# Attention operands split into fp16 halves before the transpose, and transposed by DMA instead of TensorE

## The chip, the core and the metric

The kernel runs on one core of a Trainium2 chip. The metric is the device time of one execution in microseconds (us). A core has five engines that run at the same time, each through its own list of instructions in order: TensorE (PE in the profile, with its weight loads as PEld), VectorE (DVE), ScalarE (ACT), GpSimd (POOL) and SyncE (SP), which only issues transfers here. Engines wait for each other through semaphores. SBUF is the on-chip memory (128 partitions), PSUM the accumulation memory into which TensorE writes.

## The reference, cut to what matters

The inputs are 8 sequences of 128 tokens with width 256, and as many context tokens. One layer is computed: layer norm, attention of the 128 tokens to 128 context tokens and (causally) to themselves, with 16 query heads in 4 groups that share a key and value head, then an expert layer.

```python
q = rms_norm((x @ wq).reshape(B, L, 16, 128), q_norm_w)      # likewise k (4 heads), k_ctx
q = q * cos + rotate_half(q) * sin                            # rotated query
scores = einsum('blhd,bmhd->bhlm', q, k_full) * scale + mask  # k_full: context keys, then own keys
probs = softmax(scores, axis=-1)
out = einsum('bhlm,bmhd->blhd', probs, v_full)
x = x + out.reshape(B, L, 2048) @ wo
x = x + moe(layernorm(x))                                     # 8 experts, 2 per token, and a shared one
```

## The kernel before, in words

All matrix products of the attention are made in fp16 but keep nearly fp32 accuracy: an operand is split into a high half (its fp16 rounding) and a low half (fp16 of what is left), and a product is the sum of three: high by high, low by high, high by low. ACT makes the high half, as a copy with a scale (function `copy`, line 435), and DVE the low half, as scale times source minus high half (function `low`, line 879).

The attention is a loop over the 8 sequences (`row(b, first, last)`, one for each engine; rows 1 to 6 are a hardware loop) and in it over the four groups g of four heads. One such step, 32 in all, is called a group step below; u = 4b + g counts them. What runs for a group, spread over neighbouring steps:

- `q(b, g)` projects the query two steps ahead: six matmuls of 512 columns into a PSUM bank. DVE `q_turn` multiplies by cosine and sine (lines 870, 872), GpSimd `q_add` adds the two parts into `q_rot` (line 744), ACT `q_squares` sums the squares for the RMS norm, GpSimd `q_roots` takes the root by a power (line 701).
- PE `q_turn` transposes `q_rot` in fp32, four 128x128 blocks, into the bank `turn` (line 1246). ACT `q_copy` and DVE `q_low` read it and write `qT_hi` and `qT_lo`.
- `scores(b, g)`: twelve matmuls of 256 columns and four that add the mask (lines 1267, 1289), into `sc_ps`. DVE `scores_max` reduces (line 941), ACT `exps` writes `probs` with the row sums, four activations (line 524). The root mean square of q goes into the exponent's scale. DVE `normalise` multiplies the four blocks of `probs` by the reciprocal sums (line 953).
- One step later PE `turn_probs` transposes `probs` in fp32, eight blocks (line 1300), into the two banks `pt_ps`; ACT `p_copy` and DVE `p_low` make `pT_hi` and `pT_lo`.
- `mix` multiplies them with the values (six matmuls of 512 columns, line 1310) at the end of that step; ACT `o_copy` and DVE `o_low` split the output.

Beside this, once in a row: step 0 projects the context values and the values (`vc`, `v`), step 1 carries the output projection of the row before (`out_proj`, 48 matmuls of 256 columns, line 1324) and transposes the next inputs (`turn_inputs`), step 2 projects the next row's context keys and keys (`kc`, `k`), whose norms go ACT `kc_squares`, GpSimd `kc_roots`, ACT `kc_scale`, ACT `k_squares`, GpSimd `k_roots` and `k_scale`, and step 3 transposes them on PE (`kc_turn`, `k_turn`); ACT `kc_copy` and `k_copy` and DVE `kc_low` and `k_low` split them. In step 0 the ACT order after the exponentials is `q_squares`, `v_copy`, `o_copy`, `vc_copy`; DVE `vc_low` releases the bank into which PE projects the query of group 3 (`q`, which waits for `vc_ready`), ahead of `out_proj` on PE's list.

The order on each engine is written out by hand. SP's queue holds the loads of the weights at the start, the load of `wo` (2 MB, line 406, when the last part of `wq` has been split), one load of 128 KB of context per row and two of 1 MB of expert weights, and the stores at the end.

## Time and profile before

| what | value |
|---|---|
| median of 3 runs | 377.71 us (375.49 to 378.03) |
| profiled execution, its own time | 377.97 us |
| its span, first to last instruction | 376.3 us |
| mean granted TensorE clock | 0.977 of 2.4 GHz |
| PE, DVE, ACT, POOL busy | 91%, 87%, 72%, 44% of the span |
| bytes moved by DMA | 13.49 MB |

Instructions have durations that overlap their neighbour's on the same engine by some 0.1 us, so the distance between two starts is the better price; both are used below and named. "Idle before" is the time an engine stood still ahead of the group, with what released it. Registers, branches, semaphores and the issue of DMAs do not count as busy.

### The profile page before, as it was taken

What the parts mean: (1) busy time and instruction counts of PE and PEld (TensorE: products, weight loads), DVE (VectorE), ACT (ScalarE), POOL (GpSimd) and SP (SyncE); (2) the same over time, 40 slices, a digit from 0 to 9 for tenths busy, and PEclk for the clock granted to TensorE, in tenths of its full rate; (3) what the DMA queues carried; (4) which work ended last, traced back from release to release, by engine and by line L of the source; (5) the groups of instructions that cost most, each with busy time, mean ns of one, the idle gap of its engine ahead of it and who ended that gap; (6) DMA issues with size and microseconds to landing.
All of it is one profiled execution on the core that took longest, in us unless ns stands there. A gap on an engine that the chain in (4) does not pass through costs nothing.

```text
span 376.3 us, 7781 instructions
## 1 busy us (share of the span) xinstructions
PE 343.7 (91%) x2471; PEld 237.3 (63%) x2476; DVE 325.6 (87%) x625; ACT 271.2 (72%) x913; POOL 165.8 (44%) x242
## 2 busy tenths in 40 slices
PE   6697798799999999999999999999999999998994
PEld 5373555376567665866685577567666778674572
DVE  1668999998999899899989998999899897759653
ACT  3557879676986797699759876986797567167562
POOL 3356565652754275427344443644174300334330
PEclk9788989999999999999999999999999999989999
DMA  5967000000030003000000000000000000000011
GB/s 179 379 212 223 17 0 2 1 2 14 3 111 0 14 0 111 14 1 0 0 14 0 0 0 14 0 0 0 0 0 1 2 0 2 2 0 3 22 35 57
DMA packets 11603, 13.49 MB, mean 36 GB/s; under 512 B 824, under 2 KB 9024, under 8 KB 11584
## 3 DMA queue, kind: packets, MB, share of 16 engines
q1 hardware_dynamic: 11584, 13.25, 11.0%
q8 instruction: 10, 0.16, 0.2%
q14 instruction: 9, 0.07, 0.1%
HBM read 12.20 MB, written 1.05 MB: 35 GB/s over the span
## 4 chain that ended last, share of the span: by engine, by line
PE 40%; DVE 24%; ACT 17%; issue 10%; POOL 4%; DMA 2%; SPq 1%; DVEq 1%; ACTq 0%; POOLq 0%
PE proj L1324 10%; ACT probs L524 8%; PE pt_ps L1300 5%; DVE probs L953 5%; PE proj L1157 4%; PE turn L1246 3%; DVE nmax L941 3%; DVE pT_lo L879 3%; PE o_ps L1310 3%; POOL q_rot L744 3%; PE sc_ps L1267 2%; ACT pT_hi L435 2%; DMA wq<-in_L_xattn_wq_dram 2%; ACT q_junk L468 2%; DVE q_t L870 2%
## 5 line engine op out<-in xcount | busy, mean ns | idle before, releaser
L524 ACT ACTIVATE probs<-sc_ps,nbias,q_r 128x256 f32<-128x256 f32 x128 | 70.8, 574 | 2.8 <-DVE nbias L945 2.8
L744 POOL TENSOR_TENSOR q_rot<-q_t 128x512 f32<-128x512 f32 x32 | 41.4, 1295 | 42.8 <-DVE q_t L872 42.0
L953 DVE TENSOR_SCALAR probs<-probs,rden 128x256 f32<-128x256 f32 x128 | 51.2, 461 | 1.1
L1157 PE MATMUL proj<-wq_hi,xT 128*128 128x512 f16 x128 | 40.1, 396 | 2.9 <-DVE wq_lo L863 2.9
L435 ACT ACTIVATE pT_hi<-pt_ps 128x512 f16<-128x512 f32 x64 | 34.8, 597 | 10.9 <-PE pt_ps L1300 10.9
L468 ACT ACTIVATE q_junk<-proj 128x128 bf16<-128x128 f32 x128 | 34.0, 295 | 11.7 <-DVE q_t L872 11.7
L879 DVE SCALAR_TENSOR_TENSOR pT_lo<-pt_ps,pT_hi 128x512 f16<-128x512 f32 x64 | 41.0, 682 | 0.6 <-ACT pT_hi L435 0.6
L941 DVE TENSOR_REDUCE nmax<-sc_ps 128x4 f32<-128x1024 f32 x32 | 38.9, 1214 | 1.5 <-PE sc_ps L1289 1.5
L831 POOL TENSOR_TENSOR wq<-xn_all,weight 128x512 bf16<-128x512 f32 x16 | 17.1, 1074 | 44.1 <-DVE weight L1098 23.4
L1324 PE MATMUL proj<-wo_hi,oT_hi 128*128 128x256 f16 x128 | 34.9, 273 | 0.0
L1324 PE MATMUL proj<-wo_lo,oT_hi 128*128 128x256 f16 x128 | 34.9, 273 | 0.0
L1324 PE MATMUL proj<-wo_hi,oT_lo 128*128 128x256 f16 x128 | 34.9, 273 | 0.0
L1300 PE MATMUL pt_ps<-ident,probs 128*128 128x128 f32 x256 | 34.2, 278 | 0.3
L701 POOL TENSOR_TENSOR q_r<-q_me,power 128x4 f32<-128x4 f32 x32 | 33.3, 1042 | 2.5
L435 ACT ACTIVATE qT_hi<-turn 128x512 f16<-128x512 f32 x32 | 19.5, 610 | 19.9 <-PE turn L1246 19.9
L1300 PEld LDWEIGHTS pt_ps<-ident,probs 128*128 128x128 f32 x256 | 29.5, 143 | 0.8 <-DVE probs L953 0.5
L1246 PE MATMUL turn<-ident,q_rot 128*128 128x128 f32 x128 | 19.8, 277 | 10.6 <-POOL q_rot L744 4.9
L468 ACT ACTIVATION_READ_ACCUMULATOR q_junk<-proj 128x1 f32 x128 | 28.5, 227 | 0.0
L524 ACT ACTIVATION_READ_ACCUMULATOR probs<-sc_ps,nbias,q_r 128x1 f32 x128 | 27.6, 215 | 0.0
L1310 PE MATMUL o_ps<-pT_hi,v_hi 128*128 128x512 f16 x64 | 24.3, 379 | 3.2 <-DVE pT_lo L879 3.2
L879 DVE SCALAR_TENSOR_TENSOR oT_lo<-o_ps,oT_hi 128x512 f16<-128x512 f32 x32 | 21.9, 686 | 5.8 <-ACT oT_hi L435 5.8
L1267 PE MATMUL sc_ps<-kT_hi,qT_hi 128*128 128x256 f16 x128 | 24.5, 273 | 0.5 <-ACT probs L524 0.2
(216 smaller groups left out, 920.7 us busy)
## 6 DMA issues: line engine op xcount, KB each, us to landing
wq<-in_L_xattn_wq_dram SPq DMA_DIRECT2D x4, 512.0 KB, 9.1
w<-in_L_ffn_w_dram SPq DMA_DIRECT2D x2, 1024.0 KB, 10.5
wq<-in_L_xattn_wo_dram SPq DMA_DIRECT2D x1, 2048.0 KB, 8.2
ctx_b<-in_ctx_dram SPq DMA_DIRECT2D x8, 128.0 KB, 2.1
out_dram<-x_all SPq DMA_DIRECT2D x4, 256.0 KB, 2.2
x_all<-in_x_dram SPq DMA_DIRECT2D x1, 896.0 KB, 12.3
wkc<-in_L_xattn_wk_ctx_dram SPq DMA_DIRECT2D x1, 512.0 KB, 4.2
wk<-in_L_xattn_wk_dram SPq DMA_DIRECT2D x1, 512.0 KB, 5.1
```

The lines of the kernel that those rows point to most:

```text
L435: return nc.scalar.activation(out_, in_, ACT.Copy, scale=scale)
L468: last = nc.scalar.activation(junk[:, head], bank[:, head], ACT.Square, scale=scale, accum_out=dst[:, h:h + 1])
L524: last = nc.scalar.activation(probs[:, h, :], sc_ps[:, h, :], ACT.Exp, bias=nbias[:, h:h + 1], scale=q_r[:, g, h:h + 1], accum_out=den[:, ...
L701: nc.gpsimd.tensor_tensor(r, me, power[:], ALU.pow).then_inc(root, 1)
L744: nc.gpsimd.tensor_tensor(q_rot[:], q_t1[:], q_t2[:], ALU.add).then_inc(q_added, 1)
L879: return nc.vector.scalar_tensor_tensor(out=lo, in0=src, scalar=scale, in1=hi, op0=ALU.mult, op1=ALU.subtract)
L941: nc.vector.tensor_reduce(nmax[:], sc_ps[:], AX_X, ALU.max, negate=True).then_inc(s_max, 1)
L953: last = nc.vector.tensor_scalar(probs[:, h, :], probs[:, h, :], rden[:, h:h + 1], None, ALU.mult)
L1157: last = nc.tensor.matmul(bank[:], xT[:, a, c, :], w[:, c, cols], start=(n == 0), stop=(n == 3 * DC - 1))
L1300: last = nc.tensor.transpose(pt_ps[:, a, h * P:(h + 1) * P], probs[:, h, a * P:(a + 1) * P], ident[:])
L1310: last = nc.tensor.matmul(o_ps[:], v[:, a, g * P:(g + 1) * P], p[:, a, :], start=(a == 0 and i == 0), stop=(a == 1 and i == 2))
L1324: last = nc.tensor.matmul(proj[0][:, 0:D], o[:, h // R, (h % R) * P:(h % R + 1) * P], w[:, h, :], start=(h == 0 and i == 0), stop=(h == H ...
```

## The change

Both fp32 operands are split where they lie, before they are transposed, and the fp16 halves are then transposed by DMA (SBUF to SBUF, issued from SP): per group step two transfers for the query (128x512 fp16 each) and four for the probabilities (high and low of two pairs of heads, 128x512 fp16 each), 192 in all. The transposes of PE at lines 1246 and 1300 go. `p_split` on ACT now multiplies by the reciprocal sums and rounds in one, and `p_rest` on DVE makes the low half from `probs`; so `normalise` goes, and `inv_den` computes the reciprocals and their scale. ACT `q_copy` reads `q_rot`; the low half of the query goes from DVE to GpSimd (`q_rest`), as does `k_add`. The transposed probabilities have two slots. `kc_copy` and `k_copy` move from the middle of the exponentials to their end, `kc_squares` moves behind `p_split`, `mix` of step 0 moves behind `v`. The load of `wo` is cut in four, two ahead of the first transposes and two behind the first probabilities; those of `w3` and `w2` are cut in four too.

```diff
@@ SP @@
+            def turn_q(b, g):
+                seen(sp, s_done, u)
+                for src, dst, split, landed in ((q_hi, qT_hi, q_high, d_qT_hi), (q_lo, qT_lo, q_low, d_qT_lo)):
+                    sp.wait_ge(split, u + 1)
+                    sp.dma_start_transpose(dst[:].rearrange("p (h t) -> p h t", h=R), src[:]).then_inc(landed[g % 2], 16)
+            def turn_probs(b, g):
+                if u >= 2:
+                    sp.wait_ge(pv_done, u - 1)
+                for pair in range(2):
+                    for src, dst, split in ((p_hi, pT_hi, p_high), (p_lo, pT_lo, p_low)):
+                        sp.wait_ge(split, 2 * u + 1 + pair)
+                        sp.dma_start_transpose(dst[:, slot, heads, :, :].rearrange("p h a t -> p (h a) t"),
+                                               src[:, heads, :].rearrange("p h k -> p (h k)")).then_inc(d_pT[slot][pair], 16)
+            sp.wait_ge(w_lo, G + 1)
+            load_wo(0)
+            load_wo(1)
+            turn_q(0, 0)
+            for b in range(B):
+                for g in range(G):
+                    if ahead_of(b, g, 1, b == B - 1):
+                        turn_q(*ahead_of(b, g, 1, b == B - 1))
+                    turn_probs(b, g)
+                    if (b, g) == (0, 0):
+                        load_wo(2)
+                        load_wo(3)
...
@@ ACT @@
             def q_copy(b, g):
-                act.wait_ge(q_turned, G * b + g + 1)
-                copy(qT_hi[:], turn[:], Q_SCALE / XW).then_inc(q_high, 1)
+                act.wait_ge(q_added, G * b + g + 1)
...
+                copy(q_hi[:], q_rot[:]).then_inc(q_high, 1)
+            def p_split(b, g):
+                act.wait_ge(s_rden, G * b + g + 1)
+                for pair in range(2):
...
+                    for h in (2 * pair, 2 * pair + 1):
+                        last = copy(p_hi[:, h, :], probs[:, h, :], rden[:, h:h + 1])
+                    last.then_inc(p_high, 1)
             def row(b, first, last):
-                    if g or not first:
-                        p_copy(u - 1)
-                    exps(b, g, (kc_copy, k_copy) if g == 3 and not last else ())
+                    exps(b, g)
...
+                    if g == 3 and not last:
+                        kc_copy(b + 1)
+                        k_copy(b + 1)
+                        p_split(b, g)
+                    if ahead_of(b, g, 2, last):
+                        q_squares(*ahead_of(b, g, 2, last))
+                    if g != 3 or last:
+                        p_split(b, g)
                     if g == 2 and not last:
                         kc_squares(b + 1)
-                    if ahead_of(b, g, 2, last):
-                        q_squares(*ahead_of(b, g, 2, last))
@@ POOL @@
+            def q_rest(b, g):
+                pool.wait_ge(q_high, G * b + g + 1)
...
+                nc.gpsimd.tensor_tensor(q_lo[:], q_rot[:], q_hi[:], ALU.subtract).then_inc(q_low, 1)
             def row(b, first, last, cast=None):
                 for g in range(G):
+                    if ahead_of(b, g, 1, last):
+                        q_rest(*ahead_of(b, g, 1, last))
...
                     if g == 2 and not last:
+                        k_add(b + 1)
                         k_roots(b + 1)
                         k_scale(b + 1)
                         q_roots(b + 1, 0)
@@ DVE @@
+            def inv_den(b, g):
+                nc.vector.reciprocal(inv[:], den[:]).then_inc(s_inv, 1)
+                dve.wait_ge(s_inv, u + 1)
+                nc.vector.tensor_scalar(rden[:], inv[:], P_SCALE, None, ALU.mult).then_inc(s_rden, 1)
+            def p_rest(b, g, pair):
+                dve.wait_ge(p_high, 2 * u + 1 + pair)
+                for h in (2 * pair, 2 * pair + 1):
+                    last = low(p_lo[:, h, :], probs[:, h, :], rden[:, h:h + 1], p_hi[:, h, :])
+                last.then_inc(p_low, 1)
             def row(b, first, last):
-                    if ahead_of(b, g, 1, last):
-                        q_low(*ahead_of(b, g, 1, last))
-                    if g or not first:
-                        p_low(u - 1)
                     if ahead_of(b, g, 2, last):
                         q_turn(*ahead_of(b, g, 2, last))
+                    inv_den(b, g)
+                    p_rest(b, g, 0)
...
                     if g == 3 and not last:
                         kc_low(b + 1)
                         k_low(b + 1)
-                    normalise(b, g)
+                    p_rest(b, g, 1)
@@ PE @@
             def scores(b, g):
-                pe.wait_ge(q_high, u + 1)
+                pe.wait_ge(d_qT_hi[g % 2], qT_landed(b, g))
...
-                        pe.wait_ge(q_ready, u + 1)
+                        pe.wait_ge(d_qT_lo[g % 2], qT_landed(b, g))
             def row(b, first, last):
-                    if ahead_of(b, g, 1, last):
-                        q_turn(*ahead_of(b, g, 1, last), last)
-                    if g or not first:
-                        turn_probs(b, g)
```

## Rows read from the trace of the kernel before

**Rows 1.** Page, part 1: busy us of each engine, share, instructions

```profile
PE 343.7 (91%) x2471; PEld 237.3 (63%) x2476; DVE 325.6 (87%) x625; ACT 271.2 (72%) x913; POOL 165.8 (44%) x242
```

**Rows 2.** Stretches: length; busy PE, PEld, DVE, ACT, POOL; clock, DMA share, GB/s

```profile
193.85:229.50 35.65, 34.39 (x249) 23.90 (x248) 33.99 (x68) 28.34 (x107) 15.90 (x24) 1.00 0.02 4
...
46.00:50.00 4.00, 2.22 (x13) 2.18 (x14) 3.96 (x6) 2.85 (x4) 4.00 (x2) 0.78 0.00 0
```

**Rows 3.** Groups by line, taken away: busy us, mean ns of one | idle

```profile
L953 DVE TENSOR_SCALAR probs<-probs,rden 128x256 f32<-128x256 f32 x128 | 51.2, 461 | 1.1
...
L879 DVE SCALAR_TENSOR_TENSOR pT_lo<-pt_ps,pT_hi 128x512 f16<-128x512 f32 x64 | 41.0, 682 | 0.6 <-ACT pT_hi L435 0.6
...
L435 ACT ACTIVATE pT_hi<-pt_ps 128x512 f16<-128x512 f32 x64 | 34.8, 597 | 10.9 <-PE pt_ps L1300 10.9
```

**Rows 4.** Groups by line: the nearest rows to what it adds

```profile
L435 ACT ACTIVATE x_hi<-xs 128x256 f16<-128x256 f32 x8 | 3.5, 434 | 2.9 <-DVE xs L858 2.9
...
L879 DVE SCALAR_TENSOR_TENSOR cT_lo<-turn,cT_hi 128x256 f16<-128x256 f32 x7 | 3.0, 423 | 0.0
...
L712 POOL TENSOR_TENSOR x_lo<-xs,x_hi 128x256 f16<-128x256 f32 x8 | 5.4, 670 | 27.5 <-ACT x_hi L435 27.5
...
L930 DVE TENSOR_TENSOR k_sum<-k_t 128x512 f32<-128x512 f32 x8 | 8.4, 1053 | 0.0
```

**Rows 5.** Chain that ended last, in order of time (start, us, what): PE's step 1

```profile
221.25 1.29 PE proj L1157 x6
...
222.55 5.24 PE proj L1324 x48
...
228.24 1.29 PE o_ps L1310 x6
...
229.53 0.98 PE sc_ps L1267 x9
...
231.51 0.89 PE pt_ps L1300 x8
```

**Rows 6.** Timeline of steps 2 to 3 (start us, us, engine, line)

```profile
195.59 1.23 DVE L941 TENSOR_REDUCE nmax<-sc_ps 128x4 f32<-128x1024 f32 x1 [0.21 <-PE sc_ps L1289]
...
197.87 0.57 ACT L524 ACTIVATE probs<-sc_ps,nbias,q_r 128x256 f32<-128x256 f32 x1
...
199.94 0.23 ACT L524 ACTIVATION_READ_ACCUMULATOR probs<-sc_ps,nbias,q_r 128x1 f32 x1
...
201.34 0.31 POOL L699 TENSOR_TENSOR kc_me<-kc_ss,eps_kc 128x4 f32<-128x4 f32 x1 [6.71 <-ACT kc_junk L468]
...
202.79 1.14 ACT L435 ACTIVATE kc_n<-turn,kc_r 128x128 f32<-128x128 f32 x4
...
205.10 0.20 POOL L699 TENSOR_TENSOR k_me<-k_ss,eps_k 128x4 f32<-128x4 f32 x1 [1.11 <-ACT k_junk L468]
...
206.52 1.04 POOL L730 TENSOR_TENSOR k_rot<-k_sum,k_r 128x512 f32<-128x512 f32 x1
...
208.94 1.26 POOL L744 TENSOR_TENSOR q_rot<-q_t 128x512 f32<-128x512 f32 x1
...
209.40 0.38 PE L1267 MATMUL sc_ps<-kT_hi,qT_hi 128*128 128x256 f16 x2
```

**Rows 7.** Page, part 6 and part 3: DMA issues to landing, and packets

```profile
ctx_b<-in_ctx_dram SPq DMA_DIRECT2D x8, 128.0 KB, 2.1
...
wq<-in_L_xattn_wo_dram SPq DMA_DIRECT2D x1, 2048.0 KB, 8.2
...
q1 hardware_dynamic: 11584, 13.25, 11.0%
```

**Rows 8.** Timeline: the issue of `wo`, the first scores, the last maximum

```profile
29.25 0.38 SPq L406 DMA_DIRECT2D wq<-in_L_xattn_wo_dram  x1
...
26.49 0.38 PE L1267 MATMUL sc_ps<-kT_hi,qT_hi 128*128 128x256 f16 x2
...
308.02 1.21 DVE L941 TENSOR_REDUCE nmax<-sc_ps 128x4 f32<-128x1024 f32 x1
```

More of the change, by code:

```diff
@@ L216, in xattn_moe_kernel @@
         d_wvc = sem("d_wvc")
-        d_wo = sem("d_wo")
+        d_wo = [sem(f"d_wo{i}") for i in range(4)]
         d_tab = sem("d_tab")
@@ new lines, in _ @@
+            sp.wait_ge(w_lo, G + 1)
[10 more added lines that the diff above has]
+                        load_wo(3)
+                    if g == 1 and b + 2 < B:
+                        next_ctx(b + 2)
+                    for load, r in ((load_w3, 1), (load_w2, 2)):
+                        if (b, g) in ((r, 1), (r, 2)):
+                            load(g - 1)
+                        if (b, g) == (r + 1, 0):
+                            load(2)
+                            load(3)
@@ L528, in exps @@
                 last.then_inc(s_exp, 1)
-            def p_copy(u):
-                act.wait_ge(p_turned, u + 1)
-                for a in range(2):
-                    copy(pT_hi[:, a, :], pt_ps[:, a, :], P_SCALE).then_inc(p_high, 1)
             def o_copy(u, g):
@@ L724, in k_roots, with k_add @@
                 inv_rms(k_ss[:], k_me[:], k_r[:], eps_k, k_sq, k_mean, k_root, nb + 1)
+            def k_add(nb):
+                pool.wait_ge(k_t12, nb + 1)
+                seen(pool, k_norm, nb)
+                nc.gpsimd.tensor_tensor(k_sum[:], k_t1[:], k_t2[:], ALU.add).then_inc(k_added, 1)
             def k_scale(nb):
@@ L755, in _ @@
             kc_roots(0)
+            k_add(0)
             k_roots(0)
@@ L759, in _ @@
             q_roots(0, 0)
+            q_rest(0, 0)
             q_add(0, 1)
@@ L899, in k_low @@
                     kT_hi[:, :, 1, :]).then_inc(k_ready, 1)
-            def q_low(b, g):
-                dve.wait_ge(q_high, G * b + g + 1)
-                low(qT_lo[:], turn[:], Q_SCALE / XW, qT_hi[:]).then_inc(q_ready, 1)
             def vc_low(b):
@@ L1001, in _ @@
             k_low(0)
-            q_low(0, 0)
             q_turn(0, 1)
@@ L1059, in row @@
                         o_low(u - 1, (g - 1) % G)
-                    if g == 2 and not last:
-                        k_add(b + 1)
                     if g == 0:
@@ L1410, in row @@
                         vc(b)
-                        if not first:
-                            mix(u - 1, G - 1)
-                        else:
+                        if first:
                             pe.wait_ge(w_lo, G + 2)
                         v(b)
+                        if not first:
+                            mix(b - 1, G - 1)
                     if g == 1:
```

185 lines of the change are left out of this document (87 added, 98 removed).

## The prediction

> **What bounds the kernel now.** I read the busy times first. PE has 343.7 us of 376.3 and DVE 325.6 [rows 1]; in one turn of the hardware loop, 35.65 us, PE is busy 34.39, DVE 33.99, ACT 28.34 and GpSimd 15.90 [rows 2]. So two engines are full and a third is at 80%. The chain that ended last says how they are coupled: in step 1 it stays on PE (query projection 1.29 us, output projection 5.24, mix 1.29, then the scores) [rows 5], and in steps 2 to 0 it goes through ACT, GpSimd and DVE. The reader should see in the timeline that step 2 is a relay: exponentials on ACT until 200.17, key norms on GpSimd from 201.34, `kc_n` on ACT from 202.79, GpSimd again from 205.10, `k_rot` from 206.52, and the next row's first scores on PE at 209.40 [rows 6]. An engine with less to do shortens a row only if the relay gets shorter too.
>
> **The change by engine, for one row.** PE loses 4 x 8 transposes of probabilities at 0.89 us per eight [rows 5] and 4 x 4 of the query at half that: 4 x 1.34 = 5.3 us, down to 29.1. DVE loses four pairs of `pT_lo` (8 x 0.68), four `qT_lo` of the same form (2.7), sixteen blocks of `normalise` (16 x 0.46 = 7.4) and `k_sum` (1.05) [rows 3, 4]; it gains sixteen low halves of 128x256. The nearest row is the low half of the context at 0.42 us [rows 4], which reads PSUM; both inputs now lie in SBUF. From below 0.33 (an overlap of 0.1 taken off), from above 0.63, since `k_sum` shows 1.05 for 512 elements from SBUF and half of that plus an overlap is that [rows 4]. I take 0.42: 6.8, and 0.7 for the scale of the reciprocals. DVE ends at 34.0 - 16.6 + 7.5 = 24.9. ACT loses eight `pT_hi` (8 x 0.60 = 4.8 [rows 3]) and gains sixteen 128x256 copies at 0.43 [rows 4], 6.9: up to 30.4; spaced start to start I take 0.31 each, 1.25 for a step's four. GpSimd gains four low halves of the query (twice `x_lo`, 1.3 us [rows 4]) and `k_add`: up to 22.
>
> So every engine sums to less than 31 us where a row now takes 35.5. That is the promise. The work is now nearly balanced on four engines with ACT on top, and what decides is the relay.
>
> **The relay after the change**, with the start of step 2's scores as 0; before, it is at 193.85 and the next row's at 229.5 [rows 2, 5]. Scores 1.7, maximum and bias 1.4, exponentials 2.3 (197.87 to 200.17 [rows 6]): 5.5, where it was 6.3, because ACT no longer has `pT_hi` ahead. Then ACT runs `q_squares` 1.0, **`p_split` 1.25** and only now `kc_squares` 1.0: 8.75. GpSimd's norm takes 1.5 (201.34 to 202.79 [rows 6]): 10.25, where ACT has already finished `o_copy` and waits. `kc_scale` and `k_squares`, 2.05: 12.3. It was 11.1 (205.10 less 193.85, less a hand-over). GpSimd: `k_roots` 1.45, `k_scale` 1.0, `q_roots` 1.35 and then, at the head of its step 3, **`q_rest`** 1.3, the low half of the next row's first query: 17.4. Behind it stand `q_add` and the roots of the next query. The low half must now cross a **DMA**: the plain load of 128 KB takes 2.1 us from issue to landing [rows 7]. Transposes are not in this trace. From below I take the bytes' rate, 2 MB in 8.2 us, or 0.5 us for 128 KB [rows 7]; from above 3.9, that load's 2.1 and 1.8 for smaller packets (worked out under (a)). I take 2.1, the row with the same size and issuer: 19.6. PE has waited for it since 16.6: `k_turn` could start at 14.8, behind `k_scale`, and takes 0.5, `mix` 1.3. Six score matmuls of 0.11 and the rest of the scores, 0.9: 21.2. Before, these scores started at 209.40, which is 15.55, and ended at 17.5 [rows 6].
>
> DVE alone would give 1.3 less: `p_split(3)` stands behind `k_copy`, which waits for `k_turn` (15.3), so the first `p_high` comes at 16.7, and DVE has `p_rest`, `kc_low`, `k_low`, `p_rest` and `o_low` (3.2) ahead of the maximum.
>
> Maximum and bias 1.5, exponentials 2.3: 25.0, where it was 22.1. ACT `q_squares` 1.0, `p_split` 1.25, `v_copy`, `o_copy`, `vc_copy` 0.5 each: 28.8. DVE `v_low`, `o_low` and `vc_low` end at 29.7, and that is what PE waits for before the query projection of group 3: 1.3, output projection 5.25, inputs 0.45, mix 1.3 [rows 5]: **38.1 for the row, against 35.5**. The four transposes' cover on PE is gone at this point, so their 1.3 us of step 1 brings nothing: PE stood waiting for DVE anyway. Six loop rows: +15.6 us. In row 0 DVE also has the splits of `wo`, so I count +1 there.
>
> What else the edits cost. `mix` has the transfers of the probabilities ahead of it; in step 0 the last is issued at 19.4 and PE comes at 25 (21.2 and three projections), so 5 us of landing cost nothing. Two slots make the reuse free. The reciprocals' scale is 0.2 us on DVE before `p_split`, beside `q_squares` on ACT. `k_add` (1.05 to 1.3) lies beside `kc_scale` on ACT. The pieces of `w3` and `w2` run beside compute as now.
>
> **The start.** SP issues half of `wo` first and then the first query. The issue of `wo` is at 29.25 [rows 8], some 1.1 earlier with DVE's two operations less; half of 2 MB takes 4.1 [rows 7], a transfer behind it 2.1: 34.4, against scores at 26.49 [rows 8]. PE's next work (query, context values, values) is then later by 4 to 5 us, as the next scores had waited for other things. I take +5, between 2 (DVE catches up) and 9. The last row has no keys to make and gains 2; its tail has PE work to cover the last transfers.
>
> The sum: 377.97 (the profiled execution, 0.3 above the median) + 15.6 + 1 + 5 - 2 = 397.6, so 398. A row could also be worth +1 (the query's low half finds GpSimd free earlier) or +4.5 (3.9 us landing, DVE slowed by GpSimd's reads): 387 to 414 for this case.
>
> **TensorE's clock.** PE would stand idle for over 3 us twice in a row (before the query projection that waits for `k_squares`, and before the scores, from 16.6). In this trace PE had 2.2 us of work in the 4 us from 46, and the granted clock was 0.78 there, against 1.00 in the loop row [rows 2]; part of that stretch ran at 1.2 GHz. It is in the upper bound above, since PE has slack in those steps.
>
> **The rivals.**
>
> (a) The transfers become the bound. A row has 24 of them, and they go through one queue in order: at 38.1 us per row the point is 1.59 us for one. Bulk bytes give 0.5. By packets it is 1.8: 11584 packets took 11.0% of 16 engines' 376.3 us [rows 7], 57 ns each, and 128x512 in pieces of 256 bytes is 512 packets, 32 an engine. Then 192 x 1.8 = 346, plus 30 before the first (the first scores at 26.5 and the half of `wo`) and 63 behind the last (the last maximum is at 308.0 [rows 8], its halves 5 later): 439. Each further 0.2 us adds 38. If one 128x128 block cost a whole plain transfer's 2.1 without overlap, it would be 192 x 8.4 = 1613 plus 93, 1706 us. Against (a) stands that SP is held only 0.38 us by the issue of a plain transfer, even one of 2 MB [rows 8]. The Trainium skill speaks on both sides. "DMA: Bandwidth & Descriptors" (Latency and other measured facts) gives DMA transposes 261 GB/s or more, an estimate of 0.5 us each, and (a) would not happen. "VectorE: DVE Perf Modes" (The three transpose paths) gives 1309 ns for one 128x128 block by DMA and advises TensorE where PSUM will do: block by block that is an estimate of 5.2 us per transfer, 192 x 5.2 + 93, 1091 us. No transpose is in this trace, so neither is confirmed. I give 24% for (a), with 5 of these for block by block.
>
> (b) Faster: the relay has more room than I see, and a row is the sum of the largest engine share in each step. PE in step 1 (9.8 with the scores), ACT in step 2 (8.4), 6.8 and 7.1: 32.1, 3.4 less than now. Seven rows: -24, start +5, last row -2: 357. For it speaks that DVE is 96% busy in a row and falls by a quarter; against it, that its relief lies in steps where it then waits for ACT. It decides on whether `q_rest` or `p_split` stands in the chain. 18%, from 352 to 373.
>
> (c) Both effects cancel, within 1% of 377.7: 10%. One percent is about what a measurement can tell from no change.
>
> **The numbers.** The relay case 48%, (a) 24%, (b) 18%, (c) 10%. Prediction 398 us. The range from 364 to 470 leaves out half of (b) and of (a), 2 in 10. Its own range is 387 to 414. Faster by over 1%: 18%, within: 10%, slower: 72%.
>
> **What would show it.** A row of about 38 us in the distance of the maxima of step 2; PE busy below 80% with waits for `qT_lo`'s transfer ahead of step 0's scores and for `v_lo` ahead of group 3's query projection; ACT waiting for `kc_r`; first scores at 33 or later. Wrong if PE's longest waits are on probabilities in every step with the queue busy all the time (a), or if a row is under 35 us (b).

## The result, and the profile after

| | us |
|---|---|
| before, median of 4 | 376.6 (375.45 to 378.03) |
| after, median of 4 | 446.32 (445.32 to 449.9) |
| ratio | 1.1866 [1.1781, 1.1951] |
| span after, mean granted clock | 443.6, 0.887 |

The change makes the kernel 19% slower: the direction that was forecast, at over three times the size (+69.7 us against +20). One run of `x4_qfirst` and one of `x17_two_probs`, each over 1.5% above that kernel's fastest, are left out of their medians below. The page of the changed kernel: busy times (as [rows 1]), the granted clock in 40 slices, the transfers' queue, their time to landing.

```profile
PE 332.8 (75%) x2279; PEld 227.2 (51%) x2284; DVE 289.9 (65%) x553; ACT 288.4 (65%) x977; POOL 213.1 (48%) x283
...
PEclk9968578979887988798889898969996998899999
...
q1 hardware_dynamic: 117712, 38.44, 37.0%
...
pT_hi<-p_hi SPq DMA_TRANSPOSE x64, 2.4
pT_lo<-p_lo SPq DMA_TRANSPOSE x64, 2.4
```

No engine is over 75% busy where two were at 91 and 87%. Two stretches, one loop row and its part from step 3's maximum to step 0's (columns as in [rows 2]):

```profile
196.64:239.30 42.66, 33.24 (x223) 22.50 (x222) 29.41 (x58) 30.51 (x115) 22.29 (x31) 0.88 0.33 72
205.72:217.49 11.77, 8.75 (x45) 5.68 (x46) 7.99 (x14) 9.76 (x37) 9.66 (x12) 0.71 0.31 67
```

Every engine has 9 us or more of idle time in 42.66, PE and ACT included, so the row is made of waits. The longest by sum (engine, line, what it waited for: total us, times, longest):

```profile
ACT probs L589 <- DVE nbias L1020: 71.4, 25, 8.1
DVE p_lo L963 <- ACT p_hi L491: 44.3, 32, 1.9
...
PE proj L1230 <- ACT k_junk L524: 31.1, 8, 4.5
...
PE proj L1230 <- DVE v_lo L963: 25.3, 8, 4.6
...
PE sc_ps L1318 <- DMA qT_lo<-q_lo: 17.9, 15, 2.4
```

The second is the one that the forecast had not priced: in all 32 group steps DVE stands idle for `p_hi`, 1.4 us on average, while its own next maximum is queued behind `p_lo`. The groups that answer to [rows 3, 4] (busy, mean ns | idle before):

```profile
L1230 PE MATMUL proj<-wq_hi,xT 128*128 128x512 f16 x128 | 48.9, 472 | 57.9 <-ACT k_junk L524 31.1
L963 DVE SCALAR_TENSOR_TENSOR p_lo<-probs,rden,p_hi 128x256 f16<-128x256 f32 x128 | 61.6, 532 | 45.6 <-ACT p_hi L491 44.3
L491 ACT ACTIVATE p_hi<-probs,rden 128x256 f16<-128x256 f32 x128 | 55.0, 522 | 1.3 <-DVE rden L1027 1.1
```

The relay of step 2, as [rows 6] (timeline by start; first ACT, then GpSimd, then PE, then SP):

```profile
201.36 1.73 ACT L491 ACTIVATE p_hi<-probs,rden 128x256 f16<-128x256 f32 x4
202.96 0.30 ACT L524 ACTIVATE kc_junk<-turn 128x128 bf16<-128x128 f32 x1
...
205.59 1.14 ACT L491 ACTIVATE kc_n<-turn,kc_r 128x128 f32<-128x128 f32 x4 [0.98 <-POOL kc_r L765]
```

```profile
204.26 0.20 POOL L763 TENSOR_TENSOR kc_me<-kc_ss,eps_kc 128x4 f32<-128x4 f32 x1 [6.80 <-ACT kc_junk L524]
...
211.65 1.16 POOL L820 TENSOR_TENSOR q_lo<-q_rot,q_hi 128x512 f16<-128x512 f32 x1
```

```profile
207.82 1.03 PE L1230 MATMUL proj<-wq_hi,xT 128*128 128x512 f16 x2 [4.49 <-ACT k_junk L524]
...
215.29 0.39 PE L1318 MATMUL sc_ps<-kT_hi,qT_lo 128*128 128x256 f16 x2 [0.81 <-DMA qT_lo<-q_lo]
...
227.98 1.03 PE L1230 MATMUL proj<-wq_hi,xT 128*128 128x512 f16 x2 [3.35 <-DVE v_lo L963]
```

```profile
208.35 1.19 SPq L445 DMA_TRANSPOSE qT_hi<-q_hi  x1
212.83 1.19 SPq L445 DMA_TRANSPOSE qT_lo<-q_lo  x1
214.12 1.22 SPq L456 DMA_TRANSPOSE pT_hi<-p_hi  x1
```

The timeline has the forecast relay in its order: `kc_junk` behind `p_hi`, GpSimd's norm 6.8 us idle before it, the low half of the next row's query issued at 212.83 and used at 215.29. It also has what the relay does to PE: after 4.49 and 3.35 us of standing still, pairs of the query projection take 1.03 us where they took 0.6. The granted clock of this part is 0.71: after the wait TensorE runs at the lower of its two levels (1.2 GHz), and the six matmuls take 2.74 us instead of 1.29.

One more thing in this row was in no term of the forecast's sum. The bias of step 3, `nbias`, takes 1.06 us and that of step 0 takes 0.62, where it takes 0.16 alone; each ends as the GpSimd operation beside it ends (DVE, then GpSimd):

```profile
206.97 1.06 DVE L1020 TENSOR_TENSOR nbias<-nmax,q_r 128x4 f32<-128x4 f32 x1
...
218.74 0.62 DVE L1020 TENSOR_TENSOR nbias<-nmax,q_r 128x4 f32<-128x4 f32 x1
```

```profile
206.75 1.26 POOL L793 TENSOR_TENSOR k_sum<-k_t 128x512 f32<-128x512 f32 x1
...
218.18 1.15 POOL L820 TENSOR_TENSOR q_lo<-q_rot,q_hi 128x512 f16<-128x512 f32 x1
```

Both of these operations are on GpSimd by the change. `rden` is stretched in the same way twice in the row (0.83 and 0.58 for 0.17).

### The profile page after: what moved, and what is told of

The parts are those of the page before. It is cut to its first block, busy times and chain, and to the rows that moved or that the text cites. A ratio compares the mean times of both kernels' runs of the same rounds, so it can differ in the third digit from the quotient of the medians.

```text
span 443.6 us, 7750 instructions
## 1 busy us (share of the span) xinstructions
PE 332.8 (75%) x2279; PEld 227.2 (51%) x2284; DVE 289.9 (65%) x553; ACT 288.4 (65%) x977; POOL 213.1 (48%) x283
## 2 busy tenths in 40 slices
DMA packets 117733, 38.69 MB, mean 87 GB/s; under 512 B 105416, under 2 KB 115664, under 8 KB 117712
## 3 DMA queue, kind: packets, MB, share of 16 engines
q1 hardware_dynamic: 117712, 38.44, 37.0%
HBM read 12.20 MB, written 1.05 MB: 30 GB/s over the span
## 4 chain that ended last, share of the span: by engine, by line
PE 34%; ACT 23%; DVE 22%; issue 9%; POOL 5%; DMA 4%; SPq 2%; DVEq 1%; ACTq 0%; POOLq 0%
PE proj L1370 9%; ACT probs L589 8%; PE proj L1230 7%; ACT p_hi L491 5%; DVE p_lo L963 5%; DVE nmax L1016 5%; PE sc_ps L1318 3%; DMA qT_hi<-q_hi 3%; ACT q_junk L524 3%; PE o_ps L1354 2%; DVE kT_lo L963 2%; DVE v_lo L963 2%; DVE oT_lo L963 2%; ACT k_junk L524 2%; ACT kc_junk L524 2%
## 5 line engine op out<-in xcount | busy, mean ns | idle before, releaser
L963 DVE SCALAR_TENSOR_TENSOR p_lo<-probs,rden,p_hi 128x256 f16<-128x256 f32 x128 | 61.6, 532 | 45.6 <-ACT p_hi L491 44.3
L491 ACT ACTIVATE p_hi<-probs,rden 128x256 f16<-128x256 f32 x128 | 55.0, 522 | 1.3 <-DVE rden L1027 1.1
L1230 PEld LDWEIGHTS proj<-wq_hi,xT 128*128 128x128 f16 x128 | 12.3, 112 | 73.8 <-ACT k_junk L524 32.2
L1016 DVE TENSOR_REDUCE nmax<-sc_ps 128x4 f32<-128x1024 f32 x32 | 38.9, 1217 | 13.1 <-PE sc_ps L1340 13.1
L820 POOL TENSOR_TENSOR q_lo<-q_rot,q_hi 128x512 f16<-128x512 f32 x32 | 37.2, 1163 | 7.3 <-ACT q_hi L491 7.1
L1354 PE MATMUL o_ps<-pT_hi,v_hi 128*128 128x256 f16 x128 | 37.3, 291 | 3.3 <-DVE oT_lo L963 2.7
L1318 PE MATMUL sc_ps<-kT_hi,qT_lo 128*128 128x256 f16 x128 | 25.6, 283 | 17.9 <-DMA qT_lo<-q_lo 17.9
L954 DVE TENSOR_TENSOR q_t<-proj,q_cos 128x512 f32<-128x512 f32 x32 | 22.0, 688 | 23.3 <-PE proj L1230 23.0
L1354 PE MATMUL o_ps<-pT_hi,v_lo 128*128 128x256 f16 x128 | 36.8, 287 | 0.0
L1354 PE MATMUL o_ps<-pT_lo,v_hi 128*128 128x256 f16 x128 | 36.6, 286 | 0.0
L1318 PE MATMUL sc_ps<-kT_lo,qT_hi 128*128 128x256 f16 x128 | 26.2, 285 | 0.8
```

The lines of the kernel that those rows point to most:

```text
L491: return nc.scalar.activation(out_, in_, ACT.Copy, scale=scale)
L820: nc.gpsimd.tensor_tensor(q_lo[:], q_rot[:], q_hi[:], ALU.subtract).then_inc(q_low, 1)
L963: return nc.vector.scalar_tensor_tensor(out=lo, in0=src, scalar=scale, in1=hi, op0=ALU.mult, op1=ALU.subtract)
L1016: nc.vector.tensor_reduce(nmax[:], sc_ps[:], AX_X, ALU.max, negate=True).then_inc(s_max, 1)
L1230: last = nc.tensor.matmul(bank[:], xT[:, a, c, :], w[:, c, cols], start=(n == 0), stop=(n == 3 * DC - 1))
L1318: nc.tensor.matmul(sc_ps[:, h, :], a[:, h * P:(h + 1) * P], w[:, g, :, :].rearrange("p a t -> p (a t)"), start=start, stop=False, skip_gro ...
```

## The experiments

Each ran beside the kernel before (medians 375.5 to 376.8); times are medians, ratios are to it.

**Which half of the change costs it.** `x5_only_p` keeps the query's path of before, `x6_only_q` the probabilities' path of before.

```diff
 x5_only_p: PE q_turn, ACT q_copy from `turn`, DVE q_low as before; no turn_q on SP, no q_rest
 x6_only_q: PE turn_probs, ACT p_copy, DVE normalise and p_low as before; no turn_probs on SP, no p_split
```

> Only the probabilities are split first and transposed by DMA; the query goes the old way (TensorE transposes it, ACT and DVE read PSUM), everything else as in the changed kernel. Relay theory: p_split and p_rest stay in the chain of steps 2, 3 and 0 and the slow clock stays, but the first scores of a row no longer wait for GpSimd's low half and its transfer (0.8 to 2 us a row) and the start no longer waits for a transfer behind wo (8 us): 39.5 to 42 us a row, 415 to 430 us. Rival (the query's path is the whole loss): 385 or less.

> Only the query is split first and transposed by DMA; the probabilities go the old way (normalised, transposed by TensorE, split out of PSUM), everything else as in the changed kernel. Relay theory: the key squares end 1.5 us earlier without p_split, but the query's low half still crosses GpSimd and the queue, and the start is still 7 to 10 us late: 38 to 40.5 us a row, 405 to 425 us. Rival (the probabilities' path is the whole loss): 390 or less.

Measured: 426.87 us, 1.1304 [1.1242, 1.1365], as expected; and 398.97, 1.0582 [1.0531, 1.0632], faster than expected. Less the 376.8 of before that is +50.1 and +22.2, together 72.3 against 69.7 for both: the parts add up, and the probabilities carry some 70%.

**Are the transfers the bound?**

```diff
-for src, dst, split in ((p_hi, pT_hi, p_high), (p_lo, pT_lo, p_low)):
+for src, dst, split in ((p_hi, pT_hi, p_high),):          # 16 transfers a row, not 24
```

> The changed kernel without the transfers of the probabilities' low halves: 16 transposes a row instead of 24 (the third product uses the high half twice, so this leaves out the low half of the probabilities; the split itself is still computed). Queue theory: SP is held 1.26 us by each of 24, 31 of a row's 43 us, and the waits for the query's low half come from standing behind them, so a third less gives 3 to 6 us a row, 405 to 425 us. Relay theory: the query's low half is issued when GpSimd has made it and the probabilities are never late, so a row gains at most 1 us, in step 0, and the kernel 0 to 8: 438 to 446.

Measured: 450.58, 1.1958 [1.1903, 1.2013]. A third of the transfers less gives nothing. Rival (a) is refuted: a transfer behind another holds SP 1.26 us and lands after 2.4, and 24 of them are some 30 us of a 42.66 us row.

**TensorE's clock.** Dummy matmuls into a free bank in PE's two long waits.

```diff
+if g == 1: stay_warm(18)      # ahead of the wait for k_squares
+if g == 3: stay_warm(14)      # ahead of the wait for v_lo
```

> The changed kernel with 18 dummy matmuls of 512 columns ahead of PE's wait for the key squares in step 3 and 14 ahead of its wait for the context values in step 1, both into a PSUM bank that nobody reads there (3.9 and 3.0 us, less than the two stalls of 4.5 and 3.4 us). Clock theory: the two query projections behind the stalls took 2.74 us at 1.2 GHz instead of 1.3, and two groups of transposes 0.87 instead of 0.45; all of it lies in the relay, so a loop row falls from 43.1 us by 2.3 to 2.8, the kernel from 446 to 427 to 431 us, and the mean granted clock rises from 0.887 to above 0.95. Rival (the relay is set by ACT and GpSimd alone, the slow matmuls are hidden): under 4 us less, and a row of 42 or more.

Measured: 438.21, 1.1635 [1.1548, 1.1721], clock 0.948. Half of what was expected. In the loop rows the distance of the maxima of steps 1 and 2, which was 10.2 to 13.1 us, is 10.2 to 10.5 in all of them, but that of steps 3 and 0 rose from 11.8 in most rows to 12.3 to 12.5: PE was earlier there and waited for `qT_lo` instead.

**The order of work.** Four reorderings, alone and together.

```diff
 x2_kcfirst: ACT, step 2:   kc_squares ahead of p_split
 x4_qfirst:  SP, start:     turn_q(0, 0) ahead of load_wo(0), load_wo(1)
 x7_relay:   both, and DVE k_turn, kc_low, k_low ahead of p_rest; GpSimd q_rest ahead of q_roots(b + 1, 0)
 x9_pfirst:  x7_relay, and ACT p_split ahead of q_squares in steps 0 to 2
 x8_relay_warm: x7_relay with 12 and 10 dummies as in x1_warm
```

> The changed kernel with the squares of the context keys ahead of the split of the probabilities on ACT in step 2, so that GpSimd's root runs beside the split. Relay theory: ACT no longer waits 1.0 us for the root, the key squares end 1.0 us earlier, and a row is worth 0.7 to 1.1 us less: 438 to 442 us. Rival (the row is set elsewhere, by the queue of transfers or DVE): no change beyond 1.5 us.

> The changed kernel with the transfers of the first query issued ahead of the two quarters of wo and of the wait in front of them. Theory of the start: the first scores come at 28 to 30 us instead of 32.5, and the gain survives to the end: 441 to 444 us. Rival: PE waits for the context values at 45 us anyway (3.7 us of idle time there), so nothing of it is left: 445 to 447.

> The changed kernel with five moves that shorten the relay and compute the same: ACT squares the context keys ahead of p_split; DVE rotates the keys (k_turn) ahead of p_rest in step 2; DVE makes the keys' low halves ahead of p_rest in step 3; GpSimd makes the next row's first q_rest ahead of its q_roots; the first query's transfers are issued ahead of wo. Relay theory: 1.0 from the squares (now DVE no longer holds them up), 1.3 from q_rest, 0.5 to 1 in step 3, and 6.5 us at the start: 39.5 to 41.5 us a row, 418 to 430 us. Rival (each gain turns into another wait, as the first such move did): above 436.

> The kernel before in this list with 12 and 10 dummy matmuls of 512 columns in PE's two stalls. If order and clock add up: another 1.5 to 2.5 us a row, 38 to 39.5 us, 405 to 418 us, a mean clock above 0.95. If they overlap: within 5 us of the kernel without dummies. In neither case do I expect less than 390, since ACT's p_split and DVE's p_rest remain in the chain.

> The x7_relay kernel (428.9 us) with `p_split` of steps 0 to 2 straight behind the exponentials (and `kc_squares`), ahead of `q_squares`. Theory, the ping-pong of ACT and DVE sets a step: with only the probabilities by DMA, DVE stands 5.9 us of a row idle for `p_hi`, 1.4 to 1.8 in each step, and the next maximum is queued behind its `p_lo`. `q_squares` is 0.9 to 1.0 us of that, so three steps of a row come up to 1 us earlier: rows of 39.5 to 41 where x7_relay has 42.1, 408 to 420 us, and DVE's waits for `p_hi` fall from 4.2 us a row to under 2. Rival, the steps are set by PE's waits for the squares, `kT` and `v_lo`: 425 to 432, DVE's saved wait comes back ahead of the maximum. Rival, the later `q_squares` delays GpSimd's roots and with them the bias: over 430.

Measured: `x2_kcfirst` 445.84, 1.1817 [1.1749, 1.1885], nothing, where 4 to 8 us were expected: the wait moved to DVE, whose `k_turn` stood behind `p_lo`, and ACT's `k_squares` waited 1.70 us for it. `x4_qfirst` 439.13, 1.1648 [1.1559, 1.1738], a little more gain than expected. `x7_relay` 428.91, 1.1354 [1.1288, 1.142], 10 under `x4_qfirst`: with `k_turn`, the keys' low halves and `q_rest` moved too, the swap is part of a gain. No run says which of these moves brought it. `x9_pfirst` 418.71, 1.1151 [1.1115, 1.1186], a further 10, as expected. `x8_relay_warm` 426.02, 1.1323 [1.1244, 1.1403]: the clock is worth at most 3 us once the order is mended (the single runs of the two kernels overlap, 426.0 to 429.9 and 424.8 to 429.9), so as far as these two kernels tell, it was mostly a consequence of the waits. Order and start are 28 of the 70 us.

**The query's half.** First by order, then with the first query of each row turned by PE again, so that no transfer lies between the keys' norm and the next row's scores.

```diff
 x10_q_early: x6_only_q with turn_q(0, 0) ahead of wo, and q_rest ahead of q_roots(b + 1, 0)
 x13_hybrid:  x6_only_q; group 0: PE q_turn, ACT copy and DVE low half from `turn`; groups 1 to 3 by DMA;
              kc_copy and k_copy again amid the exponentials
```

> Only the query by DMA (399.0 us), with two edits: its first transfers go ahead of `wo`, and GpSimd makes the low half of the next row's first query before the roots of its norm. If the relay into the next row is what this half of the change costs (step 3 to step 0 takes 11.9 us there against 7.7 before), the low half comes 1.2 to 1.35 us earlier in each of seven rows, 8 to 9 us, and the start gives the 4 to 7 us it gave in x4_qfirst: 383 to 388 us. Rival, the roots are then late for the bias of step 0 and give it back: 391 to 396 (the start's part alone). Rival, the landing of the transfer, 2.4 us, is counted from the end of `k_scale` anyway and nothing moves but the start: as the first rival.

> Only the query by DMA, but the first query of each row is turned by PE and split from PSUM by ACT and DVE as before, queries 1 to 3 go by DMA, and the two key copies stand amid the exponentials of step 3 as before. PE keeps one of four query turns. If the 22 us of the query's part lie in the relay into the next row and in the start, both are gone: rows 34.5 to 36 where before has 35.5, 370 to 382 us in all, and no wait for a transfer over 0.5 us. If they lie in GpSimd's extra work (three low halves of 1.16 us and `k_add` 1.27 a row, with DVE held beside them), rows stay near 37.9: 390 to 398. PE has 2 us less to do in a row; if PE's work were what bounds the kernel before, this version would be 10 to 14 us faster than it, 363 to 367.

Measured: 385.46, 1.0262 [1.0223, 1.03], and 377.5, 1.0047 [1.0021, 1.0073], both as expected. The start and the place of `q_rest` gave back 13.5 of the query's 22 us. The rest came back with the first query's turn on PE; since `x13_hybrid` also puts the key copies back amid the exponentials, how the 8 us divide between the two isn't shown. A loop row of `x13_hybrid` (columns as above):

```profile
195.86:231.63 35.77, 33.14 (x236) 22.43 (x235) 31.91 (x63) 28.47 (x107) 20.34 (x28) 1.00 0.12 26
```

PE has 1.2 us less to do than in [rows 2], DVE 2.1, and the row is no shorter than 35.65: neither was what set it. The suspect is the keys' relay, of which one link was still late (`kc_squares` behind `q_squares`: it starts 5.4 us behind the maximum of step 2, and 4.5 in the kernel before). The next two change that link, and then take `k_add` off GpSimd.

```diff
 x14_hybrid_kc:  x13_hybrid, ACT step 2: kc_squares ahead of q_squares
 x15_hybrid_add: x14_hybrid_kc, k_add on DVE ahead of step 3's maximum
```

> x13_hybrid (377.5 us) with one swap on ACT in step 2: `kc_squares` ahead of `q_squares`, as in the kernel before. In x13_hybrid the rows are 35.8 us with 2 us less on PE; the first of the context keys' squares starts at 201.23 there against 200.04 before, and step 3 to step 0 takes 9.8 us against 7.7. Theory, the relay of the keys sets the row: each of seven rows comes 0.9 to 1.2 us earlier, 369 to 372 us, about 1.5% under the kernel before. Rival, GpSimd's order (`q_add`, then `k_add`, ahead of the keys' roots) holds the relay anyway: its wait is 0.3 us behind ACT's, so 0.3 us a row are the least that would be left, 375. Rival, the row is set elsewhere: 377.

> x14_hybrid_kc with `k_add` back on DVE, where the kernel before has it (ahead of the maximum of step 3). GpSimd's 1.28 us leave the relay between the two norms; DVE gets 1.2 us. If GpSimd's queue holds the relay by 0.3 to 1.3 us once ACT is earlier: 1 to 5 us under x14_hybrid_kc, 365 to 370. Rival, DVE's maximum of step 3 is then 1.2 us later and holds the exponentials, within which the key copies stand: same as x14_hybrid_kc or up to 4 us slower.

Measured: 369.22, 0.9822 [0.9794, 0.985], and 368.48, 0.9811 [0.9786, 0.9836]. One swap on ACT, which starts `kc_squares` 1.35 us earlier in the row, makes each loop row 1.24 us shorter and the kernel 8.3 us: the keys' relay does set the row. **Both versions beat both kernels**, the one before by 1.8 and 1.9%; what the second adds can't be told from nothing. A row of `x14_hybrid_kc`:

```profile
156.00:190.54 34.54, 33.15 (x236) 22.42 (x235) 32.02 (x64) 28.39 (x107) 21.46 (x30) 1.00 0.13 27
```

**GpSimd beside DVE.** Four spare products (SBUF to SBUF, 128x512, nothing reads them) in GpSimd's idle time of step 2.

```diff
+for i in range(4): nc.gpsimd.tensor_tensor(gp_junk[:, i], q_cos (broadcast), q_sin (broadcast), ALU.mult)
                         kc_roots(b + 1)
```

> The changed kernel (446.3 us) with four spare products of 128x512 on GpSimd in each row's step 2, where it stands idle for about 8 us ahead of the context keys' norm; nothing waits for them unless they outlast that idle time. Each should take 1.0 to 1.3 us. Theory, DVE is held beside GpSimd when both its inputs are in SBUF: `nbias` (0.16 us alone) and the four `p_lo` (1.67 us for four alone) in that stretch last until GpSimd's operation ends, 1 to 3 us longer a row, and those that read PSUM (maximum, `q_t`, `oT_lo`) keep their durations; 452 to 468 us. Rival, DVE's long operations only wait for something else: durations as before and 444 to 449.

> The kernel before (375.8 us) with the same four spare products on GpSimd as x12_gp_after, 5 us in a wait of 6.7. If DVE is held beside GpSimd by any operation without PSUM among its inputs, `nbias` (0.16 us), the second norm (0.41) and possibly `rden` stretch to the end of GpSimd's operation, 0.6 to 1.2 us each, while the maximum, `qT_lo`, `pT_lo` and `q_t`, which read PSUM, keep their durations: 2 us a row, of which DVE's 1.6 us of idle time a row can take some: 378 to 392 us. The kernel before has fewer such operations beside GpSimd than the changed one, so the ratio should be no larger than the 1.018 of x12_gp_after to the changed kernel. Rival, GpSimd's work is free in its idle time: 375 to 377.

Measured: on the changed kernel 454.51, 1.2083 [1.2044, 1.2122]; on the kernel before 386.42, 1.0303 [1.026, 1.0347]. Timeline of the first, GpSimd and DVE:

```profile
200.78 5.00 POOL L862 TENSOR_TENSOR gp_junk<-q_cos,q_sin 128x512 bf16<-128x512 f32 x4
```

```profile
201.26 0.80 DVE L1024 TENSOR_TENSOR nbias<-nmax,q_r 128x4 f32<-128x4 f32 x1
201.99 1.43 DVE L1057 TENSOR_SCALAR xn_all<-x_all,ln_mv,ln_rs  x1
203.34 0.68 DVE L958 TENSOR_TENSOR q_t<-proj,q_cos 128x512 f32<-128x512 f32 x1
...
204.74 1.07 DVE L1031 TENSOR_SCALAR rden<-inv 128x4 f32<-128x4 f32 x1
206.78 1.68 DVE L967 SCALAR_TENSOR_TENSOR p_lo<-probs,rden,p_hi 128x256 f16<-128x256 f32 x4 [0.98 <-ACT p_hi L492]
```

`nbias` takes 0.80 us where it takes 0.16, `xn_all` 1.43 for 0.41, `rden` 1.07 for 0.17; `q_t`, with one input in PSUM, keeps its 0.68, and `p_lo`, behind GpSimd's last product, its 1.68. The three that are stretched have all their inputs in SBUF, and each ends as one of GpSimd's four products ends (1.25 us each). So they are held by GpSimd, and what reads PSUM and the reciprocal are not. The size of it in the row: loop rows of 43.6 us on average where the changed kernel has 43.1, 2.7 over five rows. In row 0 the products outlast GpSimd's idle time of 2.9 us, and the keys' norm starts 2.9 us later behind the maximum, so the 8 us aren't all the price of held operations. The expectation for the kernel before came out in number but not in place: its loop rows are 35.7 us against 35.5, and 9 us are lost between the maxima of step 2 of row 0 and of row 1 (45.13 to 94.91, against 48.16 to 88.94 before). There GpSimd isn't idle ahead of the keys' norm: the norm starts 12.0 us behind the maximum, where it started 6.9 behind it, so the products push it back by their own 5 us. This run's ratio, the larger one against the expectation, therefore says little on held operations; its durations do.

**The probabilities' half.** The same reorderings with only the probabilities by DMA; then two buffers for `probs`, so that `p_lo` leaves the path to the next maximum; then no `p_lo` at all.

```diff
 x16_p_early:   x5_only_p; kc_squares, then p_split right behind exps; k_turn, kc_low, k_low ahead of p_rest
 x17_two_probs: x16_p_early; probs[2]; p_rest(u - 1) behind scores_max(u); exps(u) waits for p_rest(u - 2);
                p_split(u) waits for p_rest(u - 1), since p_hi has one buffer
 x18_no_rest:   x16_p_early; no p_rest, no pT_lo; mix reads pT_hi a third time
```

> Only the probabilities by DMA (426.9 us) with the order of work of x9_pfirst where it bears on them: `kc_squares` and then `p_split` straight behind the exponentials, `k_turn` and the keys' low halves ahead of `p_rest`. If the loss of the probabilities' half is the ping-pong ACT, DVE, ACT of each step, most of the 5.9 us of a row in which DVE waits for `p_hi` goes: rows of 38 to 39.5 where it has 41.2, 402 to 414 us, and what is left (25 us and more over before) is the 1.7 us of `p_hi` and 1.7 of `p_lo` in series in every step against normalise alone at 1.14. Rival, TensorE's clock (0.93 there) and its waits are the cause and not the order: 420 or more.

> x16_p_early (425.4 us, only the probabilities by DMA) with two buffers for `probs`: DVE makes `p_lo` of a step behind the next step's maximum and bias, and the next exponentials no longer wait for it. In x16_p_early the scores of step 3 are done at 185.5 and the maximum starts at 188.15, behind four `p_lo` that took 3.68 us beside two operations of GpSimd; in step 0 the scores are done at 203.3 and the maximum starts at 206.94. Theory, the loss of the probabilities' half is `p_hi` on ACT and `p_lo` on DVE in series between the exponentials of one step and the maximum of the next: the maxima start as their scores are done, rows of 37 to 39.5 where x16_p_early has 40.9, 395 to 415 us. Rival, the low halves are then late for `mix` (2.5 us of transfer behind them), and PE waits for transfers where DVE waited for ACT: 418 to 435.

> x16_p_early (425.4 us) without the low half of the probabilities at all: neither `p_lo` on DVE nor its transfers; `mix` uses the high half in its place, so PE's work is the same. The exponentials wait for `p_hi` alone. It takes 8.7 us a row off DVE (33.8 of 40.9 busy there; four `p_lo` of 1.67 to 3.68) and 8 of 16 transfers. Theory, the row is the ring of ACT and DVE (maximum, exponentials, `p_hi`, `p_lo`, maximum) : most of one `p_lo` per step comes off, rows of 34 to 37, 380 to 400 us. Rival, what is left is `p_hi` on ACT in the same ring, the waits of PE for `kT` and `v_lo` and its clock, and DVE's work fits beside: 408 or more. x3_noplo, which took away the transfers alone, changed nothing, so the two together are DVE's part.

Measured: `x16_p_early` 425.44, 1.1315 [1.1279, 1.1352], a miss: nothing gained. `x17_two_probs` 462.8, 1.2265 [1.2151, 1.2379], a miss the other way, by its rival's mechanism but far beyond its range: the low halves and their transfers are then late for `mix`, in one row PE waits 3.2 us for `pT_lo`, and DVE 4.3 and 5.1 for `v_hi` and `oT_hi`. ACT's `p_hi` also waits there, 3.9 us for the reciprocals and 1.9 for a landing, so this run doesn't test the ring by itself. `x18_no_rest` 404.28, 1.0738 [1.0697, 1.078], between its two cases. In `x16_p_early` DVE's waits for `p_hi` did fall, from 5.9 to 2.4 us a row, but (its DVE, then GpSimd in that stretch):

```profile
183.94 3.68 DVE L931 SCALAR_TENSOR_TENSOR p_lo<-probs,rden,p_hi 128x256 f16<-128x256 f32 x4
187.55 0.68 DVE L931 SCALAR_TENSOR_TENSOR oT_lo<-o_ps,oT_hi 128x512 f16<-128x512 f32 x1
188.15 1.21 DVE L988 TENSOR_REDUCE nmax<-sc_ps 128x4 f32<-128x1024 f32 x1
```

```profile
184.10 1.45 POOL L794 TENSOR_TENSOR q_rot<-q_t 128x512 f32<-128x512 f32 x1
185.50 1.44 POOL L774 TENSOR_TENSOR k_sum<-k_t 128x512 f32<-128x512 f32 x1
```

Four `p_lo` take 3.68 us instead of 1.67: moved earlier, they fell beside two operations of GpSimd and gave the 2 us back, while step 3's scores had been done since 185.5. That this is why nothing was gained is argued from the trace and not shown: in `x5_only_p` `nbias` of step 3 is held instead (1.07 us), which is 0.16 here, so the net is 1 us. The rows of `x5_only_p` and `x18_no_rest`:

```profile
179.16:220.35 41.19, 32.81 (x240) 22.86 (x239) 31.19 (x62) 30.63 (x115) 18.13 (x26) 0.96 0.23 53
```

```profile
170.49:208.40 37.91, 31.34 (x240) 22.45 (x239) 23.53 (x47) 30.39 (x115) 17.90 (x26) 1.00 0.13 31
```

Taking out `p_lo` and its transfers (which alone are worth nothing, `x3_noplo`) gives 21 us of the 49. The other 28 stay with DVE at 23.5 us of 37.9: they aren't DVE's work. In this row PE still waits 2.6 us for `v_lo`, whose `v_hi` stands behind `p_hi` and `q_squares` on ACT, and 1.4 for `kc_n`. That `p_hi` in ACT's queue is the cause of all 28 is argued from these waits, not shown by a run.

## Why the prediction was right in direction and wrong in size

**Right.** The relay: `p_split` ahead of `kc_squares`, and GpSimd's `q_rest` and a transfer ahead of the next row's scores. With the scores' start as 0 (194.91 here), the exponentials end at 5.45 (forecast 5.5), `kc_squares` at 9.05 (8.75), `k_squares` at 12.69 (12.3), the query's low half lands at 20.4 (19.6), the next row's scores end at 22.1 (21.2). The removal of PE's work gives nothing, and rival (b) is refuted beyond the kernel itself: `x13_hybrid` has less work on PE and DVE in a row, and the same row. (c) and (a) are refuted too, (a) by `x3_noplo`. The landing of 2.1 us, taken from the plain load, was near: 2.4.

**Wrong: the size, in four terms.** By the maxima of step 2, the span of the profiled executions grew by 67.3: 10.3 up to row 0, 8.9 to row 1, 37.9 in five loop rows (35.54 to 43.1 each), 4.7 to row 7 and 5.6 behind it. Forecast were 5, 3.6, 13, and -2 for the last.

The step that failed is the sum of the relay from the next row's scores on. In the row shown, 42.66 us where the sum had 38.1, the 4.6 that it lacks are 0.9 up to the end of those scores (22.1 for 21.2), 2.4 from there to `vc_low` (10.9 for 8.5) and 1.3 from `vc_low` to the next step 2 (9.7 for 8.4). The sums by engine came out for ACT (30.51, forecast 30.4) and GpSimd (22.29, forecast 22), not for DVE (29.41, forecast 24.9) and PE (33.24, forecast 29.1, at a granted clock of 0.88). Of DVE's 4.5, 2.4 are held operations (item 2), and 1.2 come from what was taken off: 15.3 us of busy time in the row before, not 16.6.

1. "ACT `q_squares` 1.0, `p_split` 1.25" was priced once as work in a sum, not as a ring, that is a round from ACT to DVE and back that every step goes through. DVE's queue has the next maximum behind `p_rest`, and `p_rest` waits for ACT in all 32 steps (44.3 us). I priced DVE ahead of the maximum in one step only (3.2 us in step 3) and said that DVE alone "would give 1.3 less". From the next row's scores to `vc_low` it took 10.9 us (22.1 to 33.0) where I had 8.5: by the timeline an estimate of 0.5 for `oT_lo` ahead of the maximum, 0.5 for the held `nbias`, 0.35 for `p_split`, and 1.1 for the low halves behind `p_hi` and ahead of `v_lo`. `x18_no_rest` gives 21 us for DVE's part of the ring, with only the probabilities by DMA, and `x9_pfirst` 10 for the place of `p_split` in it; the same place gave nothing in `x16_p_early`. Also `p_split` itself is 1.6 us by its spacing, not 1.25: I had taken 0.31 for a copy that takes 0.40.
2. "DVE slowed by GpSimd's reads" stood in the upper bound only, and for the wrong operation. In the loop row the low halves cost what I took: 6.93 us for sixteen, 6.8 in the sum. What is held in the row is `nbias` and `rden`, by 2.4 us together in the row shown, of which `nbias` (1.4) lies ahead of the exponentials; these had no term. What the change takes off DVE was held in part too: `k_sum` takes 1.18 us in a row of the kernel before, and 0.68 to 0.71 in all eight rows of `x11_gp_before`. So my upper bound for `p_lo`, from 1.05 for `k_sum`, was the price of a held operation. The four `p_lo` of a step are held, at 2.7 to 3.7 us instead of 1.67, where a run moves them beside GpSimd (`x2_kcfirst`, `x7_relay`, `x9_pfirst`, `x16_p_early`), and in the changed kernel above all in row 0, where two of them cover the whole split of `wo` (first DVE, then GpSimd):

```profile
78.13 4.68 DVE L963 SCALAR_TENSOR_TENSOR p_lo<-probs,rden,p_hi 128x256 f16<-128x256 f32 x2
```

```profile
78.35 4.18 POOL L883 TENSOR_TENSOR wo_lo<-wq,wo_hi 128x2048 f16<-128x2048 f32 x1
```

   In the kernel before the same split holds `nbias` (first DVE, then GpSimd):

```profile
69.33 2.18 DVE L945 TENSOR_TENSOR nbias<-nmax,q_r 128x4 f32<-128x4 f32 x1
```

```profile
67.02 4.46 POOL L798 TENSOR_TENSOR wo_lo<-wq,wo_hi 128x2048 f16<-128x2048 f32 x1
```

   Held time is 3.8 us now and was 2.0, so some 2 of the 8.9 us of row 0 are an estimate for it. The Trainium skill had the rule, and I didn't use it: "SBUF — State Buffer" (Who interferes with whom) says that a DVE instruction with two SBUF inputs and a GpSimd instruction that reads SBUF exclude each other for the whole instruction. `x12_gp_after` and the rows above agree, with 0.80 for 0.16 and 4.68 for 0.9. One kind of GpSimd operation doesn't fit it, the root (see the last section).
3. TensorE's clock: "It is in the upper bound above, since PE has slack in those steps." Step 1 has none. Its query projection took 2.74 us instead of 1.29, twice a row, and `x1_warm` gives 8 us for it. With the relay mended it is worth at most 3.
4. The start: +5 for the first scores was right (they came at 32.54, 6 later), but `x4_qfirst`, which takes the transfers out from behind `wo`, gives only 7.2 of the 10.3 and 8.9. That the last row gains 2 was wrong in sign: it has the same ring in each step.

The range of the relay case alone (387 to 414) missed by 32 us, because the first three were counted as hidden or as "upper bound" and the last row was given a gain. That 446 lies inside the wide range, 364 to 470, is luck: its upper part was there for rival (a), which didn't happen. Of the 48 us that the forecast lacks, 25 lie in the five loop rows, 12 in the last row and behind it, and 5 each in the start and in row 0.

## What to carry to other kernels

When an operation moves from one engine to two others (here a transpose on PE to a split on ACT and DVE ahead of a transfer), sum the ring that each step goes through (maximum, exponential, split, low half, maximum), with what is queued between the links, and not only the busy times; here four balanced engines that wait for each other in turn were slower than two full ones. Look for the one link that the loop's next turn hangs on: here a swap of 1 us on ACT was worth 8 us, and taking three of four query transposes off PE was worth nothing without it. Price a DVE operation whose inputs all lie in SBUF by what GpSimd does beside it.
